# Two pieces of a slot change places in a fused attention and sign-weight layer: the normalised x on ACT, the first maxima on TensorE

## The reference

```python
x = x + attention(layernorm(x))          # 16 heads of 16, SEQ 1024, D 256, 8 batches
x = x + layernorm(x) @ sign(weight).T

# attention
q, k, v = (x @ W.T + b for each of q, k, v)
scores = einsum("bqhd,bkhd->bhqk", q, k) * 0.25
mask = (j <= i) & (j >= i - 128)         # a window of 128 keys back
attn = softmax(where(mask, scores, -10000.0)) + 1e-9
out = einsum("bhqk,bkhd->bqhd", attn, v) @ Wo.T + bo
```

## Time and profile before

| | |
|---|---|
| time, median of 3 runs | 806.22 us (798.45 to 813.16) |
| profiled execution | 802.16 us, its span 800.4 us |
| TensorE busy | 707.4 us (88%), weight loads 596.4 us (75%) |
| VectorE busy | 494.1 us (62%) |
| ScalarE busy | 493.4 us (62%) |
| GpSimd busy | 459.0 us (57%) |
| mean granted TensorE clock | 0.965 of full speed |
| scores, 448 exponentials L543 | 596 ns each |

### The profile page before, as it was taken

The page is one execution under the profiler, slowest core; times in us unless marked ns, Lnnn a source line. Parts: engine busy times, 40 slices in busy tenths (PEclk is TensorE's granted clock), DMA queues, the critical chain, the costliest instruction groups (busy, mean ns, idle before and its releaser), DMA issues.

```text
span 800.4 us, 31430 instructions
## 1 busy us (share of the span) xinstructions
PE 707.4 (88%) x13076; PEld 596.4 (75%) x13076; DVE 494.1 (62%) x1044; ACT 493.4 (62%) x1061; POOL 459.0 (57%) x649
## 2 busy tenths in 40 slices
PE   4478999899999999999988999998999999999985
PEld 3366877777788777778777777877777887778773
DVE  4555665666666666666566656666656666666634
ACT  3257675666666666676657666566666666566651
POOL 7835664576646556556555655555664645655763
PEclk9789999999999999999999999999999999999999
DMA  4977565675566557566766755774655766754431
GB/s 117 112 100 122 87 113 106 106 125 105 108 108 115 112 98 120 99 107 114 117 110 104 122 106 90 115 119 94 119 101 97 122 105 103 121 104 91 79 51 41
DMA packets 94940, 83.73 MB, mean 105 GB/s; under 512 B 10416, under 2 KB 94800, under 8 KB 94800
## 3 DMA queue, kind: packets, MB, share of 16 engines
q1 hardware_dynamic: 93440, 80.42, 59.5%
q10 hardware_dynamic: 1360, 1.31, 0.5%
HBM read 18.22 MB, written 8.39 MB: 33 GB/s over the span
## 4 chain that ended last, share of the span: by engine, by line
PE 68%; ACT 9%; DVE 9%; issue 6%; DMA 1%; SPq 1%; ACTq 0%; DVEq 0%
PE gc L830 16%; PE sc L962 14%; PE pv L980 14%; PE ga L830 6%; PE ga L991 5%; PE mx L919 4%; DVE nmax L682 4%; PE mx L925 3%; DVE k_lo L670 3%; ACT xn L480 3%; ACT u L601 2%; ACT prob L543 2%; PE gc L845 2%; ACT k_hi L510 2%; PE gb L1020 2%
## 5 line engine op out<-in xcount | busy, mean ns | idle before, releaser
L543 ACT ACTIVATE prob<-sc 128x512 f32<-128x512 f32 x448 | 264.0, 596 | 186.3 <-PE sc L962 184.4
L962 PE MATMUL sc<-q_stack,k_stack 128*128 128x256 f32 (+1 forms) x1024 | 227.9, 314 | 40.6 <-ACT prob L543 38.4
L682 DVE TENSOR_REDUCE nmax<-mx 128x6 f32<-128x960 f32 x188 | 195.4, 1040 | 95.4 <-PE mx L925 93.9
L962 PEld LDWEIGHTS sc<-q_stack,k_stack 128*128 128x128 f32 x1024 | 158.9, 195 | 76.6 <-ACT prob L543 47.5
L429 POOL TENSOR_SCALAR ve<-mv 128x1 f32<-128x1 f32 x64 | 14.1, 221 | 245.2 <-DVE mv L774 245.2
L980 PE MATMUL pv<-prob,v_ones 128*32 128x128 f32 x3840 | 147.0, 280 | 0.5 <-issue 0.4
L416 POOL TENSOR_SCALAR_AFFINE_SELECT prob<-prob 128x1024 f32<-128x1024 f32 x128 | 139.7, 1092 | 13.0 <-ACT prob L545 13.0
L413 POOL TENSOR_SCALAR_AFFINE_SELECT prob<-prob 128x1024 f32<-128x1024 f32 x112 | 122.4, 1093 | 41.9 <-ACT prob L543 41.7
L980 PEld LDWEIGHTS pv<-prob,v_ones 128*32 128x32 f32 x3840 | 94.2, 110 | 26.2 <-issue 1.5
L925 PE MATMUL mx<-k_max,q_stack 16*32 16x160 bf16 x4008 | 70.7, 231 | 0.8 <-issue 0.8
L662 DVE SCALAR_TENSOR_TENSOR q_lo<-gc,bq,q_hi 128x256 fp32r<-128x256 f32 x64 | 28.0, 479 | 50.1 <-ACT q_hi L499 50.1
(11 more groups left out here) (141 smaller groups left out, 1425.5 us busy)
## 6 DMA issues: line engine op xcount, KB each, us to landing
q_stack<-q_hi SPq DMA_DIRECT2D x128, 128.0 KB, 4.2
k_stack<-k_hi SPq DMA_DIRECT2D x128, 128.0 KB, 4.6
xs<-x SPq DMA_DIRECT2D x32, 256.0 KB, 4.5
q_stack<-q_lo SPq DMA_DIRECT2D x64, 128.0 KB, 4.6
k_stack<-k_lo SPq DMA_DIRECT2D x64, 128.0 KB, 4.8
xr<-x SPq DMA_DIRECT2D x64, 128.0 KB, 2.0
out<-x SPq DMA_DIRECT2D x64, 128.0 KB, 2.0
k_max<-k SPq DMA_DIRECT2D x64, 64.0 KB, 2.6
```

The costliest lines, as they stand in the source:

```text
L543: a.activation(prob[:, own:nxt + 1:nxt - own, 2 * f:2 * f + 2, :], sc, ACT.Exp, scale=SCALE).then_inc(exp_done, 1)
L682: v.tensor_reduce(nmax[:, n % 2, :].rearrange("p (r h) -> p r h", r=C)[:, :, h0:h0 + m], banks[:, :, 0:WIN * m].rearrange("p r (h k) -> p ...
L962: last = mm(sc_bank[f % 2][:, 2 * P * j:2 * P * j + q], k_stack[:, h, ak:ak + P], q_stack[:, h % HB, P * t:P * t + q], start=True, stop=True)
```

## The change

In ACT's slot `norm1` moves from behind exponential 6 to ahead of it, and `nmax_part` from ahead of exponential 1 to behind it. In TensorE's slot `max_scores` 0 and `prob_v` 0 move ahead of score pair 1, and `turn_max` moves behind score pair 1. No instruction is added or removed.

```diff
@@ ACT, slot @@
                 now, part = parts(b, t)
                 if now:
                     exp(b, t, 0)
+                    exp(b, t, 1)
                 if part["nm"]:
                     nmax_part(*part["nm"])
                 if now:
-                    exp(b, t, 1)
                     exp(b, t, 2)
@@ ACT, slot @@
                 if part["tqv"]:
                     q_part(*part["tqv"])
-                if now:
-                    exp(b, t, 6)
                 if part["ln"]:
                     norm1(*part["ln"])
+                if now:
+                    exp(b, t, 6)
@@ TensorE, slot @@
                 if now:
                     scores(b, t, 0)
-                if part["nm"]:
-                    turn_max(*part["nm"])
-                if now:
-                    scores(b, t, 1)
                 if mx:
                     max_scores(*mx, 0)
                 if pv:
                     prob_v(*pv, 0)
+                if now:
+                    scores(b, t, 1)
+                if part["nm"]:
+                    turn_max(*part["nm"])
                 if op:
                     turn_u(*op)
```

More of the change, by code:

```diff
@@ L590, in slot @@
                     q_part(*part["tqv"])
+                if part["ln"]:
+                    norm1(*part["ln"])
                 if now:
                     exp(b, t, 6)
-                if part["ln"]:
-                    norm1(*part["ln"])
                 if part["pv"]:
```

## The result

The changed kernel took 755.93 us (median of 4 runs, 751.29 to 758.38), the kernel before 806.97 (798.45 to 813.16): ratio 0.9394, 95% interval 0.9298 to 0.949. It is 51 us faster. The forecast was 748 us, in a range of 738 to 764. The profiled execution took 751.29 us, the fastest of the four, with a span of 749.5 us, against 802.16 and 800.4.

A forecast was written before the change was run, and what follows sets the result against it. The prediction took TensorE, 88% busy, as the bound, with its odd-slot pauses before score pair 1 to be won. From 802.2 us it took 43.1 for pauses, 1.2 last batch and 10 clock: 747.9 us, range 738 to 764.

The forecast's parts named there:

- The pause and its releaser: In odd slots TensorE's score pair 1 waits for ACT's exponential 7, delayed by x: 38.4 us in 33 waits.
- 1.54 us a slot: Pause cost, turn of the maxima to turn of u, 2.96 against 1.42 us; 28 slots make 43.1 us.
- with no wait left, the stretch stays at 1.42 us: On TensorE, from the old place of the turn of the maxima to the turn of u, in the new order.
- what becomes late: List of what the later copy of the turned maxima could delay: x2 transposes, ACT's exponential 2, the maxima's DMA on SP.
- No wait at the x2 transposes: The copy of the turned maxima frees their bank in time, by 0.17 us; loss taken as 0.
- The k_max DMA: Odd-slot first maxima need it 1.8 us earlier; 0 to 0.2 us wait at t = 7, none taken; slower rival 0.02.
- a sign of being wrong: Waits for L553 at the x2 transposes, for a DMA at L919, or of pair 0 for L543.
- the other signs: In the timeline after: no idle before pair 1, L543 waits near nothing, TensorE busy 93% or more, granted clock 0.99.
- The clock: Eleven 1.2 GHz stretches behind pauses, 1.40 us each, 15.4 in all; 10 us taken; rival that they stay 0.14.
- The last batch: Three slots there without x to normalise have a smaller pause, 0.58 us over the free 1.42: 1.2 us won.
- The rule on table loads: Do all ACT functions of one table set before switching, about 2.7 us a switch; priced at zero, rival chance 0.01.
- The prediction's 151 us: Added time by the skill's figure for alternating Exp and Identity on ACT, 28 x 2 x 2.7; the prediction took zero.

The follow-up runs named there:

- The ACT edit alone: The kernel before with only `norm1` moved ahead of exponential 6, TensorE's order as before: 765.43 us, ratio 0.9511.
- the order alone: The changed kernel with `norm1` back behind exponential 6, the copy of the turned maxima still behind exponential 1: 768.66 us, ratio 0.9557.

## Why the prediction was right, step by step

- **The pause and its releaser: right.** Pair 1 waited for exponential 7, x stood in front of it, and x fits between exponentials 5 and 6. The ACT edit alone gives 0.96 us a slot and the order alone 0.79; only both take the whole pause.
- **1.54 us a slot: too much, 1.29 came.** From one pair 1 to the next without low clock inside, the kernel before takes 22.41 us (337.24 to 359.65), 23.48 (171.87 to 195.35), 23.19 (383.40 to 406.59) and 22.78 (406.59 to 429.37), so 91.86 a batch; the changed one takes 86.69. That is 5.17 us for four odd slots: 36 us in 28 slots and not 43.1. The step that was mis-sized is "with no wait left, the stretch stays at 1.42 us", and the assumption that nothing behind it waits. (The 23.48 is the shortest of its kind; the same pair of slots takes up to 24.47 elsewhere without low clock, and why is open, so that 36 us is the low end.) The loss is not spread evenly. By the starts of the next x on ACT three of the four pairs of slots gain 1.44, 1.45 and 1.57 us, and the one with the bias projection gains 0.69. There the step from score pair 3 to the maxima 1 takes 1.12 us before (first three rows) and 1.86 in the changed kernel (last three), 0.74 more:

```profile
362.38 0.48 PE L962 MATMUL sc<-q_stack,k_stack 128*128 128x256 f32 x2
362.70 0.40 PE L830 MATMUL ga<-wh_o,cb_hi 128*128 128x256 f32 x2
363.50 0.28 PE L919 MATMUL mx<-edges,ident 32*32 32x192 bf16 x8
...
340.65 0.48 PE L962 MATMUL sc<-q_stack,k_stack 128*128 128x256 f32 x2
341.63 0.48 PE L830 MATMUL ga<-wh_o,cb_hi 128*128 128x256 f32 x2 [0.50 <-DVE cx L695]
342.51 0.28 PE L919 MATMUL mx<-edges,ident 32*32 32x192 bf16 x8
```

  So of the missing 0.25 us a slot, about 0.19 is the bias projection (one odd slot of four), and most of the rest is the 0.05 us of the even slots.
- **The bias projection was overlooked.** It needs `cx`, which DVE makes behind the row maxima 0; in the slot with t = 3 DVE is still busy with the bias of the batch and the statistics when TensorE comes some 1.4 us earlier (its row maxima 0 start at 339.73, right behind the statistics, and `cx` ends at 341.48, 0.15 us before the bias projection starts). The list "what becomes late" followed ACT and SP and left DVE out.
- **No wait at the x2 transposes: right.** The copy of the maxima ends at 340.24 and the transposes start at 340.51 (the answer to 362.25 in the earlier trace rows); the margin is 0.27 us, 0.17 had been worked out.
- **The k_max DMA: right, and close.** One wait of 0.26 us in the changed kernel; half a microsecond less in the even slot was enough to bring ten. By the prediction's own list a DMA wait at L919 was a sign of being wrong; it came once in 28 slots. Of the other signs TensorE's busy share fell a point short, 92% and not 93.
- **The clock: right in kind, too cautious in size.** All eleven stretches of the steady part went (15.4 us by the forecast's own price), 10 us had been taken. The pauses bring them: they went when either edit shortened the pauses and came back when these were put back long enough, while those of 0.87 to 1.22 us brought none. That was not in the prediction, and because of it the gain of the clock comes from either edit alone.
- **The last batch: wrong in sign.** 1.2 us were to be won and 1.5 were lost. DVE's x (L763) runs 52.4 us earlier than before at the end of the steady part (684.64 against 737.01) and 50.9 earlier at the end of the last batch (744.22 against 795.10). The wait for the k_stack DMA grew from 1.54 to 2.44 us and took back what the earlier slots had won, and the stretch of low clock at 714 us stands behind it.
- **Sum.** 36 us of pauses, 15 of clock, 0.5 won in the start and 1.5 lost in the last batch make 50.6 by these rows; the profiled executions differ by 50.9. The forecast of 54.3 was 43.1 + 1.2 + 10: 7 us too much for the pauses and 3 too much for the last batch met 5 too little for the clock, so that the sum is closer than its terms, which is in part luck. The profiled run is also the fastest of the four; their median is 8 us above the forecast, inside the range.
- The rule on table loads (the Trainium skill, "ScalarE: Activation LUTs", section "Rules for kernel authors") does not bite here: in the changed kernel x starts 0.49 us behind exponential 5 and exponential 7 starts 0.48 us behind the copy of u, and no idle time stands at either place. The prediction's 151 us took each change between Exp and Identity for a switch of table sets; the rule is about switches between sets, and no row here shows one between Exp, Identity and Copy.

## What to carry to other kernels

An in-order engine that waits for another in mid-slot has room for its own work there: move what stands between its last result and the next consumer into that wait, and look up what the producer of each input leaves as margin. When a pause goes, follow every engine to the next instruction that used the pause as cover, DVE and the DMAs too, since a later edit of half a microsecond can land on a transfer that was hidden until then. And test edits alone as well: if the parts give more than the whole, they share a gain, here the clock and a part of the pause.

## What the hardware showed that was not expected

TensorE's granted clock fell from 2.4 to 1.2 GHz for about 3.4 us behind some of the pauses of 1.27 us and more (11 of 28 in one kernel, 14 of 28 in another), the more often the longer they were: 6 of 21 at 1.27 us, 5 of 7 at 1.40, 7 of 7 at 1.61 and 1.62. It fell behind none of 28 pauses of 0.87 to 1.22 us. Each fall cost 1.1 to 1.4 us, as much as the pause itself: one activation more in a slot, about 0.4 us of waiting, made this kernel 27 us slower. What decides in the cases between, where some pauses of one length have a stretch behind them and some have none, was not settled. The work in front of and behind the pauses was not varied by itself.
